# Causal scores in three units of 512 columns, value products in two fills, in a pipelined attention and expert block

## The reference

```
xn  = layernorm(x)
A   = softmax(q0 k0^T / sqrt(128)) v0 @ fc + b, residual, layernorm     # one head, 128 wide
h   = rms(xn); q, k, v = heads(h wq), heads(h wk), heads(h wv)          # 16 heads of 8
q, k = rms(q) * qn_w, rms(k) * kn_w
P   = softmax over keys k <= q of (q . k) / sqrt(8)                     # causal, 256 x 256 per head
x1  = xn + (P v) @ wo   (first 32 columns of the product set to 0)
out = x + A + x1 + mixture of 4 experts(rms(x1)), top 2 of 4
```

## Time and profile before

| | us |
|---|---|
| median of 3 runs | 232.12 (230.88 to 232.77) |
| span of the profiled execution, first to last instruction | 231.3 |
| what lies around the span, against the median | 0.8 |
| PE busy over the span | 202.3 (87%) |
| ACT and DVE busy | 160.1 each (69%) |
| POOL busy | 112.9 (49%) |

### The profile page before, as it was taken

One profiled execution on the slowest core, in us unless ns is written; L12 is line 12 of the kernel. 1 busy time (PEld: TensorE's weight loads), 2 busy tenths in 40 slices (PEclk: granted clock), 3 DMA queues, 4 the chain that ended last, 5 costly groups with the idle time before them and its releaser, 6 DMA issues.

```text
span 231.3 us, 6236 instructions
## 1 busy us (share of the span) xinstructions
PE 202.3 (87%) x2132; PEld 145.6 (63%) x2132; DVE 160.1 (69%) x608; ACT 160.1 (69%) x310; POOL 112.9 (49%) x227
## 2 busy tenths in 40 slices
PE   0542898859999999999999999999999999997883
PEld 0311455436867787678767776867686777766563
DVE  2245059795858897789868995899489667847704
ACT  2123447745989698978898789878987998732730
POOL 3834225872572747282837282737375437506000
PEclk9999999997999999999999999999999999999999
DMA  4900100000000020002000200020000000100000
GB/s 124 389 16 11 37 3 1 4 0 0 4 0 3 3 68 6 0 3 68 0 3 6 68 4 0 3 68 4 0 3 27 23 4 0 48 0 3 23 0 27
DMA packets 7570, 6.09 MB, mean 26 GB/s; under 512 B 624, under 2 KB 7024, under 8 KB 7536
## 3 DMA queue, kind: packets, MB, share of 16 engines
q1 hardware_dynamic: 7248, 5.44, 7.5%
q10 hardware_dynamic: 288, 0.21, 0.3%
HBM read 4.60 MB, written 1.05 MB: 24 GB/s over the span
## 4 chain that ended last, share of the span: by engine, by line
PE 73%; DVE 11%; issue 5%; ACT 4%; POOL 3%; DMA 2%; SPq 0%; POOLq 0%; ACTq 0%; DVEq 0%
PE even_ps L1357 12%; PE scores_ps L1242 10%; PE pv_ps L1271 7%; PE odd_ps L1343 7%; PE a_ps L1212 6%; PE even_ps L1343 5%; PE even_ps L1387 4%; PE odd_ps L1387 3%; PE odd_ps L1369 3%; PE a_ps L1184 3%; PE pv_ps L1275 3%; PE a_ps L1286 3%; DMA first<-in_first 2%; DVE acc L1054 2%; PE a_ps L1202 2%
## 5 line engine op out<-in xcount | busy, mean ns | idle before, releaser
L325 POOL TENSOR_SCALAR_AFFINE_SELECT probs<-probs 128x512 f32<-128x512 f32 x64 | 40.3, 635 | 47.4 <-ACT probs L507 46.7
L507 ACT ACTIVATE probs<-scores_ps 128x768 f32<-128x768 f32 x64 | 49.9, 809 | 5.1 <-PE scores_ps L1242 4.9
L1242 PE MATMUL scores_ps<-qT,kT 32*128 32x128 f32 (+1 forms) x512 | 31.4, 361 | 0.3 <-ACT probs L507 0.2
L1357 PE MATMUL even_ps<-l_h,mid 128*128 128x256 f32 x128 | 30.7, 383 | 1.0 <-ACT l_h L569 1.0
L1242 PEld LDWEIGHTS scores_ps<-qT,kT 32*128 32x128 f32 x512 | 24.2, 192 | 10.4 <-issue 9.1
L1357 PEld LDWEIGHTS even_ps<-l_h,mid 128*128 128x128 f32 x128 | 23.4, 190 | 6.2 <-ACT l_h L569 2.1
L1343 PE MATMUL odd_ps<-xfT,up 128*128 128x256 f32 x80 | 22.1, 391 | 0.4 <-DVE acc L1054 0.4
L1271 PE MATMUL pv_ps<-probs,v_aug 128*32 128x256 f32 x256 | 21.3, 406 | 0.9 <-DVE pv_rows L834 0.4
L569 ACT ACTIVATE l_h<-even_ps 128x512 f32<-128x512 f32 x24 | 14.5, 606 | 8.1 <-PE even_ps L1357 7.1
L1212 PE MATMUL a_ps<-qkvT,xnT 128*128 128x384 f32 x32 | 17.5, 635 | 2.1 <-ACT qkv L543 1.5
L1343 PE MATMUL even_ps<-xfT,up 128*128 128x256 f32 x64 | 18.8, 418 | 0.0
...
## 6 DMA issues: line engine op xcount, KB each, us to landing
...
```

What stands on the lines that cost most here:

```text
L325: nc.gpsimd.affine_select(out=own, in_=own, compare_op=ALU.is_ge, fill=0.0, base=0, pattern=[[0, 2 * TILES], [1, P]], channel_multiplier=- ...
L507: nc.scalar.activation(probs[g % 2][:, 2 * half:2 * half + 2, 0:SEQ + P], scores_ps[:, 2 * half:2 * half + 2, 0:SEQ + P], ACT.Exp).then_in ...
L1242: ins = T.matmul(ps, kT[p][rows, g, kt * P:(kt + 1) * P], qT[p][rows, kt * P:SEQ], start=kt == 0, stop=kt == 1 and not searching, tile_pos ...
L1357: ins = T.matmul(ps_of(fill)[:, m * SEQ:(m + 1) * SEQ], wT[:, at_col:at_col + P], src[:, ci, :], start=(ci == 0), stop=(ci == HC - 1))
```

## The change

The masked copies change sides: `qT` is now kept four times with the rows of other heads zeroed, `kT` is plain. Then the groups can stand beside each other as moving columns over one stationary tile of keys. The scores become three units: key tile 0 with groups 0 and 1 (2 x 256 columns), key tile 1 with all four groups (4 x 128), key tile 0 with groups 2 and 3. Each is 4 matmuls of 512 columns, one per lane. The exponentials are 6 of 128x1024 in place of 8 of 128x768, over three `probs` buffers. The masks are 6: four of 512 elements, and two (key tile 1, `mask` 2 and 3) of 1024. `weigh_v` does two groups per fill, so there are two fills and two turns of 512 columns. PV0 now reads `probs` 0 and 1, and PV1 reads `probs` 1 and 2. The copies by ACT are still five per batch.

```diff
-    "pv": (("PV0", 2), ("XFT", 3), ("GATE", 3), ("PV1", 2), ("PV2", 2), ("PV3", 2), ("WO", 2)),
+    "pv": (("XFT", 3), ("PV0", 2), ("GATE", 3), ("PV1", 2), ("WO", 2)),
...
+    SCORE_UNITS = [(0, range(0, 2)), (1, range(GROUPS)), (0, range(2, 4))]
+    UNITS = len(SCORE_UNITS)
+    EXPS = HALVES * UNITS
@@ POOL @@
             def slot(t):
+                mask(t - 2, 3)
                 h0_gamma(t - 3)
-                mask(t - 2, 3)
                 v_copy(t - 1)
                 h0_beta(t - 3)
                 h0_add(t - 3)
                 mask(t - 2, 4)
                 mask(t - 2, 5)
-                mask(t - 2, 6)
-                mask(t - 2, 7)
@@ ACT @@
             def exp_unit(n, u):
-                g, half = divmod(u, HALVES)
-                wait(act, "scores_full", GROUPS * n + g + 1)
-                fill_ready(act, f"PV{(g - 2) % GROUPS}", n if g >= 2 else n - 1)
+                unit, half = divmod(u, HALVES)
+                wait(act, "scores_full", UNITS * n + unit + 1)
+                fill_ready(act, "PV0" if unit == 0 else "PV1", n - 1)
@@ DVE, slot @@
-                pv_turn(t - 2, 2)
...
-                pv_turn(t - 2, 3)
+                pv_turn(t - 2, 1)
...
-                pv_turn(t - 1, 0)
...
                 down(t - 3, 1, 2)
+                down(t - 3, 1, 3)
+                pv_turn(t - 1, 0)
+                logits_copy(t - 2)
...
-                pv_turn(t - 1, 1)
                 a0_inverse(t - 1)
                 e1_gate(t - 2)
@@ PE, scores and weigh_v @@
-                for kt in range(TILES):
-                    for lane in range(LANES):
-                        rows = slice(32 * lane, 32 * lane + 32)
-                        ps = scores_ps[:, lane, 0:SEQ] if kt == 0 else scores_ps[:, lane, SEQ:SEQ + P]
-                        ins = T.matmul(ps, kT[p][rows, g, kt * P:(kt + 1) * P], qT[p][rows, kt * P:SEQ],
+                for lane in range(LANES):
+                    rows = slice(32 * lane, 32 * lane + 32)
+                    out_ps = scores_ps[:, lane, :].rearrange("p (g q) -> p g q", q=width)
+                    ins = T.matmul(out_ps, kT[p][rows, kt * P:(kt + 1) * P], qT[p][rows, groups.start:groups.stop, queries],
...
             def weigh_v(n, pair):
-                wait(pe, "masked", UNITS * n + HALVES * (g + 1))
+                wait(pe, "masked", EXPS * n + HALVES * (2 + pair))
@@ PE, slot @@
             def slot(t):
                 qkv_project(t - 1, 1)
                 scores(t - 2, 1)
-                weigh_v(t - 2, 0)
                 q0_project(t - 1)
                 down(t - 4, 0)
                 down(t - 4, 1)
                 a0_scores(t - 2, 0)
                 xf_turn(t - 3)
+                weigh_v(t - 2, 0)
                 scores(t - 2, 2)
                 gate(t - 3)
                 up_layer(t - 3, "E1A", e1T[:, 0:HID])
                 a0_scores(t - 2, 1)
-                weigh_v(t - 2, 1)
-                scores(t - 2, 3)
                 up_layer(t - 3, "E1B", e1T[:, HID:])
                 fc_row(t - 2)
-                weigh_v(t - 2, 2)
                 up_layer(t - 3, "L1", l1T)
+                weigh_v(t - 2, 1)
                 up_layer(t - 3, "E0", e0uT)
...
-                weigh_v(t - 2, 3)
                 x_turn(t)
```

More of the change, by code:

```diff
@@ L575, in q_copy @@
                 fill_ready(act, "QKT", n)
-                wait(act, "scores_full", GROUPS * (n - 1))
-                nc.scalar.copy(qT[n % 2][:], ps_of("QKT")[:, 0:SEQ])
-            def k_copy(n, g):
+                wait(act, "scores_full", UNITS * (n - 1))
+                nc.scalar.copy(kT[n % 2][:], ps_of("QKT")[:, SEQ:2 * SEQ])
+            def q_copy(n, g):
                 if not live(n):
@@ L1225, in qk_turn, with scores @@
                 ins.then_inc(full_sem("QKT"), 1)
-            def scores(n, g):
+            def scores(n, u):
                 if not live(n):
@@ L1244, in scores @@
                 if searching:
-                    for kt in range(TILES):
+                    for k, g in enumerate(groups):
                         for lane in range(LANES):
                             rows = slice(32 * lane, 32 * lane + 32)
-                            ps = scores_ps[:, lane, 0:SEQ] if kt == 0 else scores_ps[:, lane, SEQ:SEQ + P]
-                            T.matmul(ps, head_rows[rows, g:g + 1].to_broadcast([32, P]), negT[p][rows, kt * P:SEQ],
+                            T.matmul(scores_ps[:, lane, k * width:(k + 1) * width],
+                                     head_rows[rows, g:g + 1].to_broadcast([32, P]), negT[p][rows, queries],
@@ L1250, in scores @@
                                      start=False, stop=False, tile_position=(32 * lane, 0))
                     for lane in range(LANES):
-                        own = scores_ps[:, lane, :].rearrange("p (n q) -> p n q", q=SEQ)[:, :, 0:P]
-                        ins = T.matmul(own, ident_bf[:], later_keys[:].unsqueeze(1).to_broadcast([P, TILES, P]),
+                        own = scores_ps[:, lane, :].rearrange("p (g q) -> p g q", q=width)[:, :, 0:P]
+                        ins = T.matmul(own, ident_bf[:], later_keys[:].unsqueeze(1).to_broadcast([P, len(groups), P]),
@@ L1267, in weigh_v @@
                     pe.wait_ge(s["zeros_ready"], n + 1)
[L1268 to L1276 removed]
+                for k in range(2):
+                    for lane in range(LANES):
+                        rows = ps_of(fill)[32 * lane:32 * lane + 32, :]
+                        T.matmul(rows[:, k * SEQ:(k + 1) * SEQ], v_aug[p][:, 0, GROUPS * lane + 2 * pair + k, :],
+                                 probs[2 * pair][:, lane, k * SEQ:(k + 1) * SEQ], start=k == 0, stop=False,
+                                 tile_position=(0, 32 * lane))
+                for k in range(2):
+                    g = 2 * pair + k
+                    for lane in range(LANES):
+                        rows = ps_of(fill)[32 * lane:32 * lane + 32, :]
+                        ins = T.matmul(rows[:, k * SEQ + P:(k + 1) * SEQ], v_aug[p][:, 1, GROUPS * lane + g, :],
+                                       probs[1][:, lane, g * P:(g + 1) * P], start=False, stop=k == 1,
+                                       tile_position=(0, 32 * lane))
                 ins.then_inc(full_sem(fill), 1)
@@ L1407, in find_maxima @@
                             rows = slice(32 * lane, 32 * lane + 32)
-                            ins = T.matmul(scores_ps[:, lane, g * P:(g + 1) * P], qT[p][rows, j * P:(j + 1) * P],
-                                           kT[p][rows, g, kt * P:(kt + 1) * P], start=g == 0,
+                            ins = T.matmul(scores_ps[:, lane, g * P:(g + 1) * P], qT[p][rows, g, j * P:(j + 1) * P],
+                                           kT[p][rows, kt * P:(kt + 1) * P], start=g == 0,
                                            stop=kt != j and g == GROUPS - 1, tile_position=(32 * lane, 0))
```

103 lines of the change are left out of this document (49 added, 54 removed).

## The result

| | before | after |
|---|---|---|
| median, us | 231.50 (230.54 to 232.77, 4 runs) | 260.15 (259.47 to 261.59, 4 runs) |
| ratio | | 1.129, 95% interval 1.122 to 1.135 |
| span of the profiled execution | 231.3 | 258.6 |
| steady slot | 23.82 | 27.07 |

The change makes the kernel 12.9% slower. The forecast was 249.4, range 240 to 257: right in sign, too small by 10.8. Of this 10.0 lie in the span (258.6, forecast 248.6). The rest is what lies around it: 1.7 or 1.8 us in each execution whose time and span are both known (260.31 and 258.6 here), not 0.8.

What follows compares the result with a forecast made beforehand. PE was taken as the bound, busy 23.68 of 23.80 us per slot. Slots of 25.8 (23.1 + 1.6 + 1.1), other stretches and head added 15.9, the clock 1.4: 231.3 + 17.3 + 0.8 = 249.4 us, range 240 to 257.

Steps and rivals of the forecast that it cites:

- the first hand-off: Mask 3 to PV0: the ACT and POOL road takes 13.15 us, PE's 11.54, so PE idles 1.6 each slot.
- the gate, due at 2.5, begins at 2.8: Times from PV0's start: PE could start the gate at 2.5 us, but DVE's turn of PV0 runs until 2.8.
- The 3.9: DVE's list from the first maximum to the last `down` step: 4.59 us before, less some 0.7 for moved steps.
- its 3.6: Batches 0 and 1 at the head: plus 3.6 us, of which 2.3 for batch 0 and 1.3 for batch 1.
- the 1.4 set apart for the clock: One more fall of PE's granted clock, caused by the new idle in the slots: plus 1.4 us.
- its 2.0: Stretch between batches 1 and 2: plus 2.0 us, the same as each steady slot.
- Two roads: From `x_turn` to the gate: PE's by PV0 and unit 3, due at 2.5 us; DVE's turn, due at 2.8.
- Rival D: Only the mask costs, the road to L1 being shorter than forecast: slot 24.7, time 241 us; chance 0.13.
- Rival E: The clock falls in most slots, 1.43 us in five of them: 255 us; chance 0.17.
- B: PE stays the bound: slot 23.1 us, 5 us saved, time 227; chance 0.05.
- C: Weight loads bound PE, and 64 per batch become 24: 13 us saved, time 219; chance 0.02.
- my 0.7: PE's work per slot: 0.7 us less, from units, double products and a vanished 0.18 wait, leaving 23.1.

Runs made afterwards that it cites:

- experiment 3: Changed kernel with masks 2 and 3 over 512 of their 1024 elements, part of the diagonal left unmasked: 250.29 us.
- 10: Changed kernel with POOL's order undone, gamma ahead of mask 3 again: 262.75 us.
- 4: Changed kernel with all six exponentials over 768 of their 1024 elements, the rest of `probs` constant: 254.07 us.
- 12: Changed kernel with two `down` steps moved ahead of the first Newton pass in DVE's list: 261.38 us.
- Experiment 2: Changed kernel with DVE's turn of PV0 moved up, behind the second of the last four `down` steps: 254.29 us, ratio 1.093.
- Filler: Changed kernel with extra unread 384-column matmuls in PE's idle ahead of PV0, one in batch 0, three in batch 1: 257.07 us, ratio 1.106.
- experiment 8: Kernel before, old sizes, with PV1 ahead of the gate, its turn behind the `down` steps and mask 3 ahead of gamma: 253.82 us.

## Why the prediction was right and wrong

**Right:** the direction, and the first hand-off. `x_turn` to PV0 took 13.25 (forecast 13.15), by way of exponentials of 1025 ns and masks of 1097. The profile names ACT's `xfT` as PV0's releaser, but that copy was done at 138.34 + 0.47 = 138.81 and mask 3 at 139.43; PV0 started at 139.53, and it moved with the mask in experiments 3 and 10. `L1` to `x_turn` took 6.06 (5.95), the gate to `L1` 3.86 (3.9), a unit 1.07, a turn 0.71. PE's idle before PV0 was 1.22, not 1.6, as 0.36 of it had been spent a little earlier, before the first 128-wide scores, on `q0_copy`: the three longer exponentials ahead of it push that out as well, and I had looked at them only on the way to the mask.

**The step that failed: "the gate, due at 2.5, begins at 2.8".** It begins at 3.91. I dated the turn from the first maximum, at -1.7 plus 3.9 (that is 2.2, not the 2.1 that I wrote). The maximum came at -1.40, since its scores wait those 0.36 for `q0_copy`; the list from there took 4.55. The 3.9 was the old list less four steps, as if each DVE step had a duration of its own. It has not: the larger masks, and gamma moved behind them, put POOL's row of operations 1.02 us later against the maximum (mask 3 ended 0.28 behind its start before, 1.30 now), and DVE's small steps end with them; the first alone lasts 1.03 in place of 0.36. From the end of mask 3 to the turn are 3.25 us, the same to 0.01 with a shorter mask (experiment 3), shorter exponentials (4) and another order of DVE's steps (12), and 2.56 where gamma no longer stands between (10). Experiment 2 took the turn out of the list and gave the forecast slot, 25.81. That is 27.07 - 25.8 = 1.27 a slot. In four slots it is 5.0, in 6 to 7 (where the same gate is late) 1.3 more: 6.3 of the 10 us of span that the sum lacked. Nearly all of the rest is the head, 6.1 above its 3.6, less the 1.4 set apart for the clock and 1.5 that the stretch 1 to 2 stayed below its 2.0.

The Trainium skill states this rule in "SBUF — State Buffer", SBUF: two separate sides: VectorE and GpSimd share a pair of ports, a VectorE operation with two inputs in SBUF and a GpSimd operation that reads SBUF exclude each other, and whoever starts second is blocked for the whole of the other. The trace agrees in every place shown: steps with both tensors in SBUF end 0.07 to 0.08 behind POOL's operation, `down`, with its product in PSUM, keeps its 0.30. I had not weighed it, and it spoke against this change.

**Two roads** run from `x_turn` to the gate, and the later one counts. The forecast had both, the gate due at 2.5 by PV0 and unit 3, at 2.8 by DVE's turn; it is the second that it had 1.1 too short, because it dated it from the maximum and not from mask 3 and POOL's operations behind it. That experiment 2 met 25.8 to the second place is partly luck: its 13.23 + 2.51 + 10.07 were 13.15 + 2.8 + 9.85 in the forecast. Rival D (only the mask costs, 24.7 a slot) is out: no version with PV0 ahead of the gate came below 25.36, even with half masks.

**The head** cost 7.8 in batch 1, not 1.3, with three falls more, not one. My 1.4 was for one fall in a steady slot; all came in the head, where PE's waits are of 1.4 to 2.6 us. Filler shows about 3 us for three of them. Half masks, with one fall, had the third unit of batch 1 at 53.58, 7.5 sooner than after. How the 6.5 missing there divide between falls and longer waits isn't settled. They may feed each other, since at half clock PE's longer rows (a unit 1.72 at 35.94, 1.14 in a steady slot) arrive late at the next hand-off; this is not shown.

**Rival E** (a fall in most slots) did not happen in the steady part of the kernel after, with 3.5 us of idle in five pieces per slot. It happened in experiment 8, with 0.56 and 1.68 of idle. The Trainium skill, "TensorE: Matmul & The Clock Gate", HAM oscillation, describes a kernel that loses the clock at each pause of its loop. Experiment 8 looks like that, with one fall a slot; the steady slots of the kernel after, at a granted clock of 1.00, do not. **B and C** are out, as the slot grew. PE's own work was a smaller saving than I had: 23.55 busy against 23.68, not 23.1, though the single steps cost what I said; 0.18 of my 0.7 had been a wait, the rest no run splits. The scores' weight loads fell from 24.2 to 7.9 us while a unit took what its columns cost.

```profile
...
L1246 PEld LDWEIGHTS scores_ps<-qT,kT 32*128 32x128 f32 x192 | 7.9, 193 | 7.7 <-issue 7.3 <-ACT qT L594 0.3
...
```
